# A graph network on one core: the one-hot mask of the self-edge pick, in PSUM instead of SBUF

## The reference

```python
ht = jnp.einsum('nd,rdo->nro', h, W_rel[l])          # 16 messages for each node
msg = ht[src, etype]                                 # one of them for each edge
h_rel = jax.ops.segment_sum(msg, dst, num_segments=n) + h @ W_loop[l] + b_rel[l]
z = (h @ W_gat[l]).reshape(n, H, DH)
e = jax.nn.leaky_relu(el[src] + er[dst], 0.2)        # el, er: z times two vectors
alpha = softmax of e over the edges of a destination
h_gat = jax.ops.segment_sum(alpha[:, :, None] * z[src], dst, num_segments=n)
hc = jnp.concatenate([h_rel, h_gat], axis=1) @ W_fuse + b_fuse
h = jax.nn.relu(hc * gate if l == 0 else hc)
```

## Time and profile before

| | us |
|---|---|
| median of 3 runs | 3562.57 |
| lowest and highest | 3561.27, 3563.65 |
| the profiled execution | 3565.3 |
| its span, first to last instruction | 3563.6 |
| POOL busy (share of the span) | 2508.9 (70%) |
| VectorE busy | 2690.2 (75%) |
| PE busy | 685.9 (19%) |
| ScalarE busy | 431.6 (12%) |

### The profile page before, as it was taken

One profiled execution on the slowest core, in us unless ns is written; L12 is line 12 of the kernel. 1 busy time (PEld: TensorE's weight loads), 2 busy tenths in 40 slices (PEclk: granted clock), 3 DMA queues, 4 the chain that ended last, 5 costly groups with the idle time before them and its releaser, 6 DMA issues.

```text
span 3563.6 us, 18787 instructions
## 1 busy us (share of the span) xinstructions
PE 685.9 (19%) x1897; PEld 369.1 (10%) x1897; DVE 2690.2 (75%) x3453; ACT 431.6 (12%) x813; POOL 2508.9 (70%) x2595
## 2 busy tenths in 40 slices
PE   8932111112222221111111111122000000000000
PEld 5421000001111110000000000011000000000000
DVE  7637877888777874787888877787577788877786
ACT  3530111111111111011111111111000000000000
POOL 1457777777777764777777777775677777777766
PEclk9975555555555555555555555555555555555555
DMA  7774444444444453444444444454344333333332
GB/s 272 311 238 128 133 142 150 149 147 147 142 143 145 142 160 102 127 143 132 149 149 148 148 139 137 143 160 142 106 107 107 106 106 107 106 107 107 105 99 78
DMA packets 140988, 499.73 MB, mean 140 GB/s; under 512 B 43525, under 2 KB 50250, under 8 KB 131362
## 3 DMA queue, kind: packets, MB, share of 16 engines
q0 software_dynamic: 127776, 438.20, 41.9%
q1 hardware_dynamic: 13186, 61.26, 4.5%
HBM read 334.80 MB, written 164.52 MB: 140 GB/s over the span
## 4 chain that ended last, share of the span: by engine, by line
POOL 37%; issue 31%; DVE 17%; DMA 7%; PE 4%; POOLq 2%; DVEq 1%; SPq 1%; ACT 1%; ACTq 0%
POOL meta_nat L614 16%; POOL late L614 13%; POOL scratch L614 6%; DVE own_sum L1483 3%; DVE acc L1439 3%; DMA late<-table,stage_mid 3%; DVE late L1435 2%; DMA meta_nat<-table,stage_head 2%; DVE own_rows L1476 2%; PE ps_table L918 1%; DVE meta_nat L1435 1%; DMA scratch<-table,stage_tail 1%; DVE scratch L1435 1%; PE ps_cnt L951 1%; POOLq L389 1%
## 5 line engine op out<-in xcount | busy, mean ns | idle before, releaser
L614 POOL DMA_INDIRECT meta_nat<-table,stage_head x1200 | 1195.0, 996 | 390.5 <-issue 368.3
L614 POOL DMA_INDIRECT late<-table,stage_mid x624 | 591.7, 948 | 190.1 <-issue 187.4
L614 POOL DMA_INDIRECT scratch<-table,stage_tail x579 | 547.8, 946 | 226.0 <-issue 223.8
L1057 PE MATMUL ps_mix<-ident,hr 128*128 128x128 f32 x75 | 35.6, 475 | 2162.3 <-DVE hg L1463 2162.3
L816 ACT ACTIVATE ps_cnt<-logit 128x68 f32<-128x68 f32 x183 | 42.3, 231 | 2824.7 <-DVE logit L1421 2824.7
L1439 DVE TENSOR_REDUCE acc<-meta_nat 128x132 f32<-128x2244 f32 x75 | 306.6, 4088 | 7.7
L1429 DVE TENSOR_REDUCE acc<-meta_nat 128x128 f32<-128x2048 f32 (+1 forms) x75 | 288.2, 3843 | 0.0
L1081 PE MATMUL ps_table<-wrel,hT 128*128 128x512 f32 x400 | 268.2, 833 | 0.0
L1057 PEld LDWEIGHTS ps_mix<-ident,hr 128*128 128x128 f32 x75 | 13.7, 182 | 2210.9 <-DVE hg L1463 2210.9
L1439 DVE TENSOR_REDUCE acc<-scratch 128x132 f32<-128x2112 f32 (+1 forms) x69 | 213.5, 3094 | 7.1
L1429 DVE TENSOR_REDUCE acc<-scratch 128x128 f32<-128x2048 f32 (+1 forms) x69 | 208.9, 3028 | 8.8
(11 more groups left out here) (261 smaller groups left out, 1920.2 us busy)
## 6 DMA issues: line engine op xcount, KB each, us to landing
table<-rows SPq DMA_DIRECT2D x25, 2080.0 KB, 7.1
meta_nat<-table,stage_head POOLq DMA_INDIRECT x1225, 2.8
late<-table,stage_mid POOLq DMA_INDIRECT x624, 2.8
scratch<-table,stage_tail POOLq DMA_INDIRECT x579, 2.8
meta<-meta_ranked SPq DMA_DIRECT2D x1, 2449.5 KB, 15.1
wrel<-in_L_gnn_W_rel POOLq DMA_DIRECT2D x2, 1024.0 KB, 13.3
meta_nat<-in_x SPq DMA_DIRECT2D x1, 832.0 KB, 19.6
table<-rows,stage_id POOLq DMA_INDIRECT x50, 7.8
```

Source lines behind the costliest of these rows:

```text
L614: pool.indirect_dma_start(out=slots[b][:, k, :], out_offset=None, in_=table[l % 2], in_offset=bass.IndirectOffsetOnAxis(ap=index, axis=0)) ...
L1057: pe.transpose(mix[0], hr[:], ident[:])
```

## The change

The mask is copied once to PSUM, into the bank `ps_place`, after the first tile of layer 0, behind a wait for the last `er` row (so that nothing else still uses the bank) and ahead of a wait for the copy itself. L1476 then reads the copy. Everything else stays as it is.

```diff
         ps_er = [ps_z[:, 0:H + D], ps_place[:, 0:H + D]]
+        own_mask = ps_place[:, 0:T * R].rearrange("p (t r) -> p t r", r=R)
...
                     v.tensor_tensor(own_rows[:], rows[0][:, :, 0:D],
-                                    own_hot[:, bass.ds(t, 1), :].rearrange("p o (r f) -> p (o r) f", f=1
-                                                                           ).to_broadcast([P, R, D]), ALU.mult
+                                    own_mask[:, bass.ds(t, 1), :].rearrange("p o (r f) -> p (o r) f", f=1
+                                                                            ).to_broadcast([P, R, D]), ALU.mult
                                     ).then_inc(s_own_rows, 1)
...
                 tile(l, 0, first=True)
+                if l == 0:
+                    dve.wait_ge(s_er, T)
+                    v.tensor_copy(own_mask, own_hot[:]).then_inc(s_own_type, 1)
+                    dve.wait_ge(s_own_type, 2)
                 with dve.Fori(1, T) as t:
```

## The result

The kernel with the mask in PSUM takes 3532.81 us (median of 4 runs, 3529.55 to 3538.75), against 3563.11 of the kernel before on the same chip (4 runs, 3561.27 to 3566.29). The ratio is 0.9916, with a 95% interval of 0.9899 to 0.9933: about 30 us less.

What follows compares the result with a forecast made beforehand. POOL, held in its gathers beside L1476, was taken to set the pace in the long tiles, VectorE in the middle ones. 12.7 + 11.5 + 4.65 + 0.7 = 29.6 us off the 3562.57 median gives 3533.0 us, range 3524 to 3545.

Steps and rivals of the forecast that it cites:

- two cases side by side: Layer 0 tile: gather beside L1435 (one input PSUM) takes 0.95 us, beside L1476 (both SBUF) 1.93; should return to 0.95.
- Rival 1: Gathers beside L1476 stay held, by writing own_rows or reading rows, not the second SBUF input: 3562.6 us, chance 0.06.
- 300 to 870, 12.7 us: Layer 0 stretch, in us of the trace, where POOL sets the pace: 14.0 us of stalls, 12.7 gained.
- The stall that was to be cut short: Stall at 815.04, 2.13 us: POOL then waits for a buffer VectorE releases, so only 0.85 is gained.
- 1440 to 2010, 11.5 us: Layer 1 stretch where POOL sets the pace: 12.5 us of stalls, about 1.0 swallowed by a wait, 11.5 gained.
- The middle stretches, 0 of 28.3: 870 to 1263 and 2010 to 2440, VectorE sets the pace: of 28.3 us of stalls nothing comes off.
- rival 3: All held time comes off, the middle stretches' 28.3 us too: about 3505 us, chance 0.05.
- The last tiles, 3.65 + 1.0: 1263 to 1330 and 2440 to 2465, short tiles with the stall on the path: 4.65 us gained.
- The layers' ends, 0.7 + 0: Layer 0's last store, held beside L1476: gain between 0 and 1.46 us, 0.7 taken; nothing for layer 1's end.
- L1477 itself and the copy, 0: The multiply (L1476 before) costs the same with its mask in PSUM; the one-time copy, 0.45 us, is covered: 0.
- rival 2: VectorE pays for the PSUM read, L1476 taking 4.15 us, 1.87 more: 3577 us, chance 0.03.
- Layer 2, "as long as before": Layer 2, where L1476 does not run: expected to be as long as before, only earlier.

Runs made afterwards that it cites:

- The experiment on tiles 13 to 21: Mask from PSUM only in tiles 13 to 21 of layers 0 and 1, from SBUF elsewhere, against the kernel before: 3567.23 us, ratio 1.0008.
- the kernel with the extra multiply out of PSUM: Changed kernel plus an unused self-edge multiply per tile from tile 1 in layer 2, mask from PSUM: 3545.04 us, 0.9944 to the kernel before.

## Why the prediction was right

**What holds POOL.** The prediction read it from two cases side by side, L1435 and L1476. It held: no gather beside the multiply is long any more, and the other input in PSUM does the same. Rival 1 is out by that. What the prediction took for the condition, a second SBUF input, is narrower than what the runs show (the copy); for this change that made no difference.

**300 to 870, 12.7 us.** The two traces start this stretch 0.6 to 0.7 us apart, after behind, already ahead of the copy (head gathers at 268.40 against 267.74), and end it 11.4 apart: 12.0. VectorE's twelve waits for `late` up to there, which answer to the earlier trace rows (one more falls into the window here), went from 70.9 us to 56.0:

```profile
...
DVE raw L1412 <- DMA late<-table,stage_mid: 56.0, 12, 8.7
...
```

The stall that was to be cut short is cut: POOL now waits 1.86 for the buffer there, where the earlier trace rows had 0.30.

```profile
...
837.43 0.94 POOL L626 DMA_INDIRECT meta_nat<-table,stage_head  x1 [1.86 <-DVE acc L1440]
...
```

**1440 to 2010, 11.5 us.** Layer 1 begins 16.6 ahead (its first logits at 1383.72 against 1400.29) and its long tiles end 27.5 ahead: 10.9. The wait of 1.55 near 1990 has become 2.42, so the stall ahead of it was swallowed.

```profile
...
1964.19 0.94 POOL L615 DMA_INDIRECT meta_nat<-table,stage_head  x1 [2.42 <-DVE acc L1440]
...
```

**The middle stretches, 0 of 28.3.** The lead is 11.4 when the first begins, 10.9 when it has passed, and in layer 1 27.5 and 27.2 (2388.99 against 2361.80). The experiment on tiles 13 to 21 shows the same by itself, and rival 3 is out. The freed time has become POOL's wait, as in the tile of the earlier trace rows, which had 1.46:

```profile
...
947.24 1.00 POOL L700 DMA_INDIRECT table<-rows,stage_id  x1 [0.30 <-issue]
...
949.45 0.14 DVE L1399 CAST stage_tail<-meta 128x15 uint32 x1
...
951.06 0.96 POOL L615 DMA_INDIRECT scratch<-table,stage_tail  x1 [2.83 <-issue]
...
```

**The last tiles, 3.65 + 1.0.** From 10.9 to 15.0 in layer 0, 4.1; from 27.2 to 28.2 in layer 1, 1.0. **The layers' ends, 0.7 + 0.** Layer 0's end gave 1.6 (a lead of 16.6 behind one of 15.0) and layer 1's 0.5 (the first logits of layer 2 at 2506.36 against 2535.02, a lead of 28.7 behind one of 28.2). The last store of layer 0 takes 0.98 against the 2.45 of the earlier trace rows; that of layer 1 takes 0.98 against 1.44, a stall that the prediction left out.

```profile
...
1353.08 0.98 POOL L700 DMA_INDIRECT table<-rows,stage_id  x1 [19.96 <-ACT meta L851]
1361.96 0.98 POOL L615 DMA_INDIRECT meta_nat<-table,stage_head  x1 [7.89 <-issue]
...
```

From the end of this store to the next layer's first gather are 7.89 us, and from the end of the long one of before as well (1370.66 to 1378.56): in this pair the full 1.47 counted, not half. Other traces have up to 8.9 for that distance, so one pair does not fix it to a few tenths.

**L1477 itself and the copy, 0.** 2280 against 2283 ns: the nearest row, L1435, was the right one, and rival 2 is out. The copy takes 571 ns (0.45 was expected from the rate of other operations) and lies in covered time.

**Layer 2, "as long as before".** It was 2.3 us longer in this execution: the lead falls from 28.7 to 26.4. All its gathers are slightly longer, 349.61 / 368 = 0.950 for the head's against 0.946; the kernel with the extra multiply out of PSUM, which has the change too, has 348.35 for the same 368. That speaks for the execution, which stands 6 us above its own median, as the cause, and against the change; neither is shown.

**The sum.** The terms, 29.6, are met by the medians (30.3, with an interval of 24 to 36) rather than by the two traces (26.4). Part of the closeness is luck: the two long stretches gave 1.3 us less than forecast, the ends of the layers 1.4 more, and these nearly cancel.

## What to carry to other kernels

An instruction can cost nothing on its own line and still be expensive: look at what a neighbour on the other engine takes while it runs, and compare two places that differ in one operand. Then price the stall by who waits for whom in that stretch: 59.5 us of held gathers were worth about 30, since in the tiles paced by VectorE a freed POOL only waits longer. Where an operand also exists in PSUM, reading it there is free here (2280 against 2283 ns), and shortening VectorE's own step pays where the stall did not.

## What was not expected of the hardware

A copy from SBUF to SBUF with a single input held POOL's indirect transfers as well, 1.38 to 1.90 us instead of 0.946, though for a shorter time than the multiply, and it is itself shorter (1262 against 2303 ns). The two hold differently. In the kernel before, none of the 42 indirect DMAs that were under way when a multiply began is longer for it (0.96 us at most), and all 46 gathers that begin inside one end 0.82 us after it. The copy also holds gathers that had begun up to 0.51 us ahead of it, and these end 0.12 us after it; those that begin over 0.1 us into it end 0.82 after. A strided sum of the same 2048 elements does not: gathers beside L1484 take 0.95.

Short multiply-adds that read PSUM run closer together than their own durations say: the group by form has 342 ns for one, but twelve of them take 3.19 us, 0.27 each.

```profile
...
L1489 DVE SCALAR_TENSOR_TENSOR own_rows<-ps_table,own_hot,own_rows 128x128 f32<-128x128 f32 x600 | 159.2, 342 | 0.0
...
```
